# A fourth pair by seven products in the later blocks, with its mixed weights made in the first block

## What is computed

```python
xn = layernorm(x)                                  # (2048, 1024)
s = silu(xn @ w_gate.T)                            # 2752 columns
s[the 1376 smallest |s| of each token] = 0
a = (s * (xn @ w_up.T)) @ w_down.T
h = relu(xn @ up_w) ** 2                           # 2048 columns
shared = h @ down_w
route = sum of the two largest of xn @ gate_w
routed = ((xn @ fc1_w) @ expert_w * route) @ fc2_w
y = x + a + layernorm(shared + routed) * gamma + beta
```

## Time and profile before

| | before |
|---|---|
| median of three runs | 2335.38 us |
| the profiled execution, its own time | 2335.83 us |
| its span, first to last instruction | 2333.7 us |
| granted TensorE clock | 1.000 |
| TensorE matmul busy | 2317.7 us, 99% |
| VectorE busy | 1634.8 us, 70% |
| ScalarE busy | 1086.9 us, 47% |
| GpSimd busy | 829.3 us, 36% |
| chain that ended last | TensorE 93%, DMA 3%, VectorE 1%, SyncE's queue 1%, GpSimd 1% |
| moved by DMA | 558.43 MB, mean 239 GB/s |

### The profile page before, as it was taken

How to read it: one execution, slowest core, us unless ns; L and a number is a source line. 1 busy time by engine, 2 the same in 40 slices (tenths; PEclk the granted TensorE clock), 3 DMA queues, 4 the chain that set the end, 5 groups by cost and what they waited for, 6 DMA issues and landing times.

```text
span 2333.7 us, 27748 instructions
## 1 busy us (share of the span) xinstructions
PE 2317.7 (99%) x10504; PEld 1927.2 (83%) x10504; DVE 1634.8 (70%) x1810; ACT 1086.9 (47%) x1253; POOL 829.3 (36%) x682
## 2 busy tenths in 40 slices
PE   8999999999999999999999999999999999999999
PEld 6888888888877888888888888888888888888887
DVE  4349999976265989897334598898723568989850
ACT  3247776223233787722124387761213448785110
POOL 5467878796444021123024321304004413030500
PEclk9999999999999999999999999999999999999999
DMA  7798878878898666665778766665667865556555
GB/s 277 280 394 294 292 245 311 293 243 310 287 363 302 206 196 191 204 201 180 234 237 277 249 194 193 195 209 189 207 219 255 279 221 195 193 192 214 180 190 180
DMA packets 191047, 558.43 MB, mean 239 GB/s; under 512 B 20161, under 2 KB 29377, under 8 KB 190913
## 3 DMA queue, kind: packets, MB, share of 16 engines
q1 hardware_dynamic: 190912, 556.65, 71.0%
HBM read 429.62 MB, written 126.94 MB: 238 GB/s over the span
## 4 chain that ended last, share of the span: by engine, by line
PE 93%; DMA 3%; DVE 1%; SPq 1%; POOL 1%; ACT 0%; issue 0%; DVEq 0%; ACTq 0%
PE bank L945 30%; PE bank L947 30%; PE bank L946 30%; PE bank L965 2%; DMA mixed_w<-mixes 1%; DMA split_w<-w 1%; DMA w<-mixed_w 1%; PE bank L956 1%; POOL w L732 0%; SPq L565 0%; SPq L569 0%; PE bank L1038 0%; PE bank L1039 0%; DMA raw<-w_gate_dram 0%; POOL w L735 0%
## 5 line engine op out<-in xcount | busy, mean ns | idle before, releaser
L1292 DVE TENSOR_SCALAR_CACHE_REDUCE junk_v<-mag,cand 128x2816 bf16<-128x2816 f32 x248 | 780.3, 3146 | 8.8
L786 ACT ACTIVATE junk_s<-mag,cand 128x2816 uint8<-128x2816 f32 x248 | 655.4, 2643 | 222.2 <-DVE cand L1284 195.7
L945 PE MATMUL bank<-w,tok 128*128 128x512 f32 (+1 forms) x952 | 365.8, 384 | 1.8 <-DMA w<-split_w 1.7
L947 PE MATMUL bank<-w,tok 128*128 128x512 f32 (+1 forms) x952 | 364.3, 383 | 0.0
L946 PE MATMUL bank<-w,tok 128*128 128x512 f32 (+1 forms) x952 | 364.1, 382 | 0.0
L732 POOL TENSOR_TENSOR w<-raw,w 128x512 fp32r<-128x512 f32 (+1 forms) x196 | 268.1, 1372 | 77.5 <-ACT w L774 67.8
L945 PE MATMUL bank<-w,prod_t 128*128 128x512 f32 x672 | 269.4, 401 | 0.0
L947 PE MATMUL bank<-w,prod_t 128*128 128x512 f32 x672 | 262.8, 391 | 0.0
L946 PE MATMUL bank<-w,prod_t 128*128 128x512 f32 x672 | 261.9, 390 | 0.0
L945 PE MATMUL bank<-tok,w 128*128 128x512 f32 x640 | 249.0, 389 | 0.0
L946 PE MATMUL bank<-tok,w 128*128 128x512 f32 x640 | 249.0, 389 | 0.0
(11 more groups left out here) (149 smaller groups left out, 3728.3 us busy)
## 6 DMA issues: line engine op xcount, KB each, us to landing
w<-split_w SPq DMA_DIRECT2D x516, 512.0 KB, 3.5
split_w<-w SPq DMA_DIRECT2D x192, 512.0 KB, 4.9
w_more<-split_w SPq DMA_DIRECT2D x60, 512.0 KB, 5.2
w<-mixed_w SPq DMA_DIRECT2D x108, 256.0 KB, 3.5
rows<-x_dram SPq DMA_DIRECT2D x32, 512.0 KB, 4.9
raw<-w_down_dram SPq DMA_DIRECT2D x44, 256.0 KB, 3.9
raw<-w_up_dram SPq DMA_DIRECT2D x40, 256.0 KB, 3.1
w<-split_w SPq DMA_DIRECT2D x24, 392.0 KB, 3.5
```

Of the source, the lines that this page charges most:

```text
L786: act.activation(junk_s[:, :, :], mag[:, :, t, :], ACT.Sign, scale=-1.0, bias=cand[:, t:t + 1], accum_out=cnt[:, t:t + 1]).then_inc(counte ...
L945: pe.matmul(out, left[0], right[0], start=first, stop=False)
L947: return pe.matmul(out, left[1], right[0], start=False, stop=last)
L1292: dve.tensor_scalar(junk_v[:, :, :], mag[:, :, t, :], cand[:, t:t + 1], float(1 - (GATED - KEPT)), ALU.is_lt, ALU.add, accum_out=cnt[:, t: ...
```

## The change

In blocks 1 to 3 up 0 and up 1 become a fourth pair (`PAIRS`, `FAST`), right behind the third. The later blocks have 260 granules instead of 248: gate 5, four pairs (8 to 119), latent (120), hidden (128), routed (144), shared 0 and 1 (152), hidden 2 and 3 (168), shared 2 and 3 (184 to 199), up 2 and 3 (200), out (216 to 259). Block 0 keeps its 212.

- The search of a later block begins at 101: bit 0 at 101, then 108, 115, 122, and from there every 2.75 granules to 197; its end is at 199. In block 0 it takes one granule more every eight bits.
- Up 0 and up 1 lie where `hidden` and `squares` will lie. SyncE stores them to `spilled_u` (two of 1 MB) at granule 123 and loads them back at 199; ScalarE's first read of hidden waits for the stores. VectorE gives them their signs with two more `sign_up`, ahead of masks 0 and 1, at 205 and 207.
- S3 and S4 go to `acc`. Their splitting moves to granules 12 and 10, and waits until the last outputs of the block before are stored.
- Sets 8 to 15, of the third and fourth pair, are made in block 0 by GpSimd (`late_mix`), with `raw_more` as the one buffer. Set 8 + n: its four loads at granules 38 + 9n to 41 + 9n, its subtractions at 44 + 9n, its four stores of 256 KB at 46 + 9n. The first load of a set waits until the stores of the set before have landed. The sets of block 1, and `mix_later`, are gone.
- In block 0 ScalarE rounds the high half of granules 54, 57, ... 123; GpSimd keeps the other 92.
- The low halves of the last product of pair 4 (index 3) are made by GpSimd, not VectorE.

The diff, cut to its core:

```diff
-PAIRS = [(("gate", 0), ("gate", 1)), (("gate", 2), ("gate", 3)), (("gate", GC - 2), ("up", GC - 2))]
-FAST = len(PAIRS)
+PAIRS = [(("gate", 0), ("gate", 1)), (("gate", 2), ("gate", 3)), (("gate", GC - 2), ("up", GC - 2)),
+         (("up", 0), ("up", 1))]
+
+FAST = [0, 4, 4, 4]
 FIRST_PAIRS = 2
+UP_PAIR, SPILLED_PAIR = 2, 3
 PRODUCTS = ["A11 B11", "S2 T2", "A12 B21", "S1 T1", "S4 B22", "S3 T3", "A22 T4"]
-PRODUCT_BANK = [[4, 6, 0, 2, 4, 6, 0], [2, 4, 6, 4, 6, 0, 2], [4, 6, 0, 4, 6, 0, 2]]
+PRODUCT_BANK = [[4, 6, 0, 2, 4, 6, 0], [2, 4, 6, 4, 6, 0, 2], [4, 6, 0, 4, 6, 0, 2],
+                [4, 6, 0, 4, 6, 0, 2]]
...
-        steps = _middle + _last
+        steps = [step for step in _middle + _last if step[0] not in sum(PAIRS[:FAST[b]], ())]
...
+            self.fast_at.update({last + 2: (FAST[b] - 1, 5), last + 3: (FAST[b] - 1, 6)})
+            self.signs_at = {end["fast", p, q] + FAST_LAG + 3: (p, q) for p in range(UP_PAIR) for q in (5, 6)}
+            up_end = end["fast", UP_PAIR, 6]
+            self.signs_at[last + 4 if up_end == last else up_end + FAST_LAG + 3] = (UP_PAIR, 6)
+        if later and FAST[b] > SPILLED_PAIR:
+            first = up_end + FAST_LAG + 4
+            steps_at = [first, first + 7, first + 14]
+            steps_at += [last + 3 + (11 * k + 3) // 4 for k in range(BITS + 1 - len(steps_at))]
         else:
-            self.search_from = end[("gate", GC - 2)] + LAG + 1
-        self.search_at = {self.search_from + 3 * k: k for k in range(BITS)}
-        self.search_end = self.search_from + 3 * BITS
+            first = last + 5 if later else end[("gate", GC - 2)] + LAG + 1
+            steps_at = [first + 3 * k + (0 if later else k // 8) for k in range(BITS + 1)]
+        self.search_at = {m: k for k, m in enumerate(steps_at[:BITS])}
+        self.search_from, self.search_end = first, steps_at[BITS]
...
+        self.back_at = end[("shared", 3)] if FAST[b] > SPILLED_PAIR else None
+        read = {("up", c): self.back_at + 5 + 2 * c for c in range(2)} if self.back_at else {}
+        read.update({key: end[key] + LAG for key in end})
+        self.mask_at = {max(self.search_end + 1 + i, read.get(("up", g), 0) + 1): g
...
-GPSIMD_HI = list(range(FIRST_PLAN.search_from, FIRST_PLAN.out0))
+GPSIMD_HI = [m for m in range(FIRST_PLAN.search_from, FIRST_PLAN.out0) if m > 124 or m % 3]
...
-MIX_STORES = {26: 8, 34: 9, 46: 10, 54: 11}
+LATE_SETS = {FIRST_MIXES + n: (0, 38 + 9 * n) for n in range(2 * HALF)}
+LATE_LOADS = [{at + i: (n, i) for n, (b, at) in LATE_SETS.items() for i in range(4) if b == c} for c in range(BLOCKS)]
+LATE_AT = [{at + 6: n for n, (b, at) in LATE_SETS.items() if b == c} for c in range(BLOCKS)]
+LATE_STORES = [{at + 8: n for n, (b, at) in LATE_SETS.items() if b == c} for c in range(BLOCKS)]
...
+def vector_makes(granule):
+
+    return PRODUCTS[granule.key[2]] == VECTOR_LO and granule.key[1] < SPILLED_PAIR
...
-SUMS_LO_AT = {2: 4, 4: 3}
+SUMS_HI_AT = [{}, {10: 4, 12: 3}, {10: 4, 12: 3}, {10: 4, 12: 3}]
+SUMS_LO_AT = [{}, {10: 4, 12: 3}, {10: 4, 12: 3}, {10: 4, 12: 3}]
...
+        sums_acc = {i: [over(f"sums{i}_acc{part}", [P, HALF, 2 * P], F32R, acc_at + 8 * N * (2 * (i - 3) + part))
+                        for part in range(2)] for i in (3, 4)}
+        assert 32 * N == TILES * HID * 4
+
+        def sums_of(b, i):
+
+            return sums_acc[i] if i > 2 and FAST[b] > SPILLED_PAIR else sums[i]
...
+        def late_place(n, i):
+
+            return (raw_more if n in LATE_AT[0].values() else raw)[:, i, :]
...
-            def load_mix(n):
+            def load_late_mix(n, i):
 
                 p, k = n // HALF, n % HALF
-                if n < FIRST_MIXES + 2:
-                    sp.wait_ge(stored, 16 * (MIX_BLOCK * 2 * TILES + 1))
+                if n == FIRST_MIXES:
+                    sp.wait_ge(mixes_made, 4 * FIRST_MIXES)
                 else:
-                    sp.wait_ge(mixes_stored[n % 2], 16 * (n // 2))
-                for i in range(4):
-                    src, width = words_of((PAIRS[p][i // 2], k + i % 2 * HALF))
-                    sp.dma_start(mix_place(n, i), src).then_inc(mix_loaded[n % 2], 16)
-
-            def store_later_mix(n):
-                sp.wait_ge(later_mixes, 4 * (n - FIRST_MIXES) + 4)
-                words = acc[:, 2 * (n % 2):2 * (n % 2) + 2, :].rearrange("p t (i n) -> p t i n", n=N)
-                sp.dma_start(mixed_w[n].rearrange("(t i) p n -> p t i n", i=2), words).then_inc(mixes_stored[n % 2], 16)
+                    sp.wait_ge(late_stored, 64 * (n - FIRST_MIXES))
+                if n in LATE_AT[1].values():
+                    sp.wait_ge(lo_ready, FIRST_PLAN.count)
+                src, width = words_of((PAIRS[p][i // 2], k + i % 2 * HALF))
+                sp.dma_start(late_place(n, i), src).then_inc(late_loaded, 16)
+
+            def store_late_mix(n, i):
+                sp.wait_ge(late_mixes, 4 * (n - FIRST_MIXES) + 4)
+                sp.dma_start(mixed_w[n, i], late_place(n, i)).then_inc(late_stored, 16)
+
+            def spill(b, c):
+
+                for q in (4, 5) if c else (2, 6):
+                    for j in range(2):
+                        bank, value = emptied(b, ("fast", SPILLED_PAIR, q, j))
+                        sp.wait_ge(bank_emptied[bank], value)
+                sp.dma_start(spilled_u[c], prod[:, 4 * c:4 * c + 4, :, :]).then_inc(spilled[c], 16)
+
+            def load_back(b, c):
+
+                sp.wait_ge(spilled[c], 16 * spills(b))
+                sp.dma_start(prod[:, 4 * c:4 * c + 4, :, :], spilled_u[c]).then_inc(up_back[c], 16)
...
-                    sp.wait_ge(mixes_stored[n % 2], 16 * (n // 2 + 1))
+                    if n < FIRST_MIXES:
+                        sp.wait_ge(mixes_stored[n % 2], 16 * (n // 2 + 1))
+                    else:
+                        sp.wait_ge(late_stored, 64 * (n - FIRST_MIXES + 1))
...
                 plan = PLANS[b]
-                if b == MIX_BLOCK:
-                    for n in MIX_LOADS.get(m, ()):
-                        load_mix(n)
-                    if m in MIX_STORES:
-                        store_later_mix(MIX_STORES[m])
+                if m in LATE_LOADS[b]:
+                    load_late_mix(*LATE_LOADS[b][m])
+                if m in LATE_STORES[b]:
+                    for i in range(4):
+                        store_late_mix(LATE_STORES[b][m], i)
+                if plan.back_at:
+                    if m == plan.fast_end + 4:
+                        spill(b, 1)
+                        spill(b, 0)
+                    if m == plan.back_at:
+                        load_back(b, 0)
+                        load_back(b, 1)
...
+            def late_mix(n):
+
+                b11, b21, b12, b22 = (late_place(n, i) for i in range(4))
+                at = 4 * (n - FIRST_MIXES)
+                pool.wait_ge(late_loaded, 64 * (n - FIRST_MIXES + 1))
+                pool.tensor_tensor(b11, b12, b11, ALU.subtract).then_inc(late_mixes, 1)
+                pool.tensor_tensor(b12, b22, b12, ALU.subtract).then_inc(late_mixes, 1)
+                pool.wait_ge(late_mixes, at + 1)
+                pool.tensor_tensor(b22, b22, b11, ALU.subtract).then_inc(late_mixes, 1)
+                pool.wait_ge(late_mixes, at + 3)
+                pool.tensor_tensor(b21, b21, b22, ALU.subtract).then_inc(late_mixes, 1)
...
-                    elif POOL_LO[g] > POOL_LO[g - 1]:
+                    if m in LATE_AT[b]:
+                        late_mix(LATE_AT[b][m])
+                    if b and POOL_LO[g] > POOL_LO[g - 1]:
...
-                if i > 2:
+                if i > 2 and FAST[b] > SPILLED_PAIR:
+                    act.wait_ge(stored, 16 * (b * 2 * TILES + 1))
+                elif i > 2:
                     act.wait_ge(bank_filled, filled(b - 1, ("out", 1, TILES - 1)))
...
                                 act.wait_ge(mixes_stored[n], 16 * (FIRST_MIXES // 2))
+                        if FAST[b] > SPILLED_PAIR and i == 0 and t == 0:
+                            for c in range(2):
+                                act.wait_ge(spilled[c], 16 * spills(b))
...
-            def sign_up(b):
-
-                ks = slice(4 * (GC - 2), 4 * (GC - 1))
-                dve.wait_ge(signs_done, b * (GC + 1) + PLANS[b].signs_before[GC - 2] + 1)
-                for j in range(2):
-                    for q in (4, 5):
-                        bank, value = emptied(b, ("fast", FAST - 1, q, j))
-                        dve.wait_ge(bank_emptied[bank], value)
+            def sign_up(b, g):
+
+                ks = slice(4 * g, 4 * g + 4)
+                dve.wait_ge(signs_done, b * (GC + 1) + PLANS[b].signs_before[g] + 1)
+                if g < 2:
+                    dve.wait_ge(up_back[g], 16 * spills(b))
+                else:
+                    for j in range(2):
+                        for q in (4, 5):
+                            bank, value = emptied(b, ("fast", UP_PAIR, q, j))
+                            dve.wait_ge(bank_emptied[bank], value)
```

(8 more changed lines are left out.)

98 lines of the change are left out of this document (41 added, 57 removed).

## The result

The changed kernel takes 2373.21 us (median of four runs, 2371.22 to 2377.07), the kernel before beside it 2335.45 (four, 2334.80 to 2336.54): a ratio of 1.016, 95% interval 1.0148 to 1.0173. It is slower by 38 us. The forecast was 2347, range 2317 to 2358; the sign was right, the size far off.

The account below looks back on a forecast made before the run. TensorE, busy 99% of the span, was taken as the bound. From 2335.8 us: -16.3 (fewer products), -4.3 (block 1's stalls), +27 (sets in block 0), +3 and +2 (new waits) gave 2347.2, stated as 2347, range 2317 to 2358.

Parts of the forecast that it names:

- Fewer matmuls, -16.3: Up chunks 0 and 1 as a fourth fast pair in three later blocks: 72 fewer matmuls, -16.3 us.
- Block 1's four stalls, -4.3: Early block 1: with the sets gone, its four TensorE stalls vanish and it looks like block 2, -4.3 us.
- Block 0, +27: Eight late sets in block 0: ring losses, first set's small lead and squarings cost +27 us, between +3 and +39.
- the ring: Block 0's late-set cycle through GpSimd, SyncE and DMA queues, one buffer: taken as 28.0 us against TensorE's 24.5 per round.
- ScalarE's third high halves: Block 0's search: every third high half, made by ScalarE behind its counts, costs nothing, with 5 us left as cover.
- The squarings add about 0.5: Block 0: GpSimd's squarings add about 0.5 us to the loss, beside the first set's 2 us.
- VectorE's wait hidden: VectorE's wait for `late_stored` at up 4 comes 15 granules after the last set, so it costs nothing.
- (a): Later blocks, granule 13: S3 and S4 halves on GpSimd delay its low half; 1 us per block, +3 us.
- (b): Later blocks' search and tail: threshold and sign passes delay the first transpose, +0.7 us per block, +2 in all.
- (c): Pair 3's low halves on GpSimd end 1.3 us before their granules; nothing, up to 1 us each block.
- The hidden and half hidden ring: Block 0 rivals: queues serve rounds quickly, about 2323 us, chance 0.31; or 26.5 us per round, 2336 us, chance 0.17.
- The rival of the 358 GB/s rule: Block 0: 358 GB/s binds mixed reads and writes, block 0 loses 43 us, time 2363 us; chance 0.03.

## Why the prediction was wrong in size

- **Fewer matmuls, -16.3.** Right: 72 fewer.
- **Block 1's four stalls, -4.3.** Right in size (with what remains, block 1 is 7.0 shorter: 5.4 of matmuls and 4.3 of stalls, less what pair 3 and others gave back), and wrong in one point: a stall of 0.2 to 0.7 us stays or comes where the first mixed weights are used, in some blocks.
- **Block 0, +27: the failed step, +52.1 measured.** The term priced the ring's excess over 24.5 us per round and took every other cost there as next to nothing: GpSimd's own time ("it fits, with 3.3 us to spare"), ScalarE's high halves, the clock. The stalls came where it said, behind the sets and ended by GpSimd, but the experiments show that a set costs TensorE time when the ring is hidden as well. Of the 52.1 us, 6.3 are ScalarE's share and 45.8 the sets; by kind, 39.1 are stalls and 12.7 half clock. The round was derived as 28.7 and then taken as 28.0. That choice was the wrong way: it was 29.6 in the set looked at and 30.2 on average. Of its legs the stores were faster (7.1 against 8.2), granules until the stores slower (4.2 against 3.4), the burst slower (13.2 against 11.8). Seven rounds lose 40 us against 24.5, so about 15 of the missing 25 are here, and part of it is the next point: the half clock behind the stalls lies within these rounds. How much of it lengthened them isn't shown.
- **Half clock, priced at nothing, 12.7 us.** The page of before, with a granted clock of 1.000, could not show it. The run with stalls of chosen length gives what was needed: 1.6 to 2.9 us for each of its stalls from 2.66 us on.
- **"As the ring doesn't contain TensorE, a lead can't cure it."** At nine granules nothing cured it, but the sentence hid the quantity that decides in general. The lead was there to be read: in the rows of before GpSimd idles 0.72 us per granule, because it is as far ahead as six slots allow, 11.3 us at granule 57, whose low half ends at 178.1 against the prediction's own 189.4 for TensorE. I read it at granules 40 and 45 alone.
- **ScalarE's third high halves at nothing, cover "5 us".** Wrong: 7.6 us without sets, 14.3 with four. They were late not behind the second count of a bit but because ScalarE's counts themselves wait for VectorE's candidate, up to 11.5 us in the changed kernel. In the changed kernel itself, with eight sets, the effect can't be told from the scatter.
- **"The squarings add about 0.5"; VectorE's wait hidden.** Wrong: VectorE waited 30.8 us in six waits for GpSimd's squares. At the end of block 0 the sign read of an up group (L1342) was late: 4.0 us of stall at 518.92 and half clock behind it. That the first made the second by way of a late search is argued, not shown (the short form of that chain, at 248.47 without sets, is in the rows above). The waits' row (us in total, times, longest):

```profile
DVE hidden L1507 <- POOL squares L823: 30.8, 6, 12.1
```

- **(a) Granule 13, +3.** No such stall. **(b) Threshold and first transpose, +0.7 per block.** 0.3 to 0.7: right. **(c) Pair 3 at nothing, at most 1 us per block.** 2.1 us of stall, 2.4 to 3.4 of time. The walk put the low halves 1.3 us ahead of their granules; it left out that the second of two counts falls between high halves. Blocks 1 to 3 gained 10.7 us where -16.3 - 4.3 + 5 = -15.6 was said: their losses were 9.9 and not 5, some 6.3 of them in pair 3, 1.5 at the first transposes, the rest mainly stalls of 0.2 to 0.5 us at the first mixed weights and pair 2's last product. The prediction named as a sign of being wrong that the first transposes don't come 3 to 5.5 us closer together; in blocks 2 and 3 they came only 2.0 and 1.7 closer.
- **SyncE waiting 5 us per round for stores, near 400 GB/s.** The rate was 315 and 300 GB/s in the two stretches with sets. SyncE waited 14.0 us in seven waits, at most 3.1: the four issues themselves take 3.6, and what was left was shorter.

```profile
SPq L629 <- DMA mixed_w<-raw_more: 14.0, 7, 3.1
```

- **Rivals.** The hidden and half hidden ring were wrong. (The quiet ring adds up to 3.4 + 6.5 + 8 + 5.3 = 23.2 us, where the prediction has 23.8; nothing hangs on it.) The rival of the 358 GB/s rule came out nearest in time (2363), not for its reason: the trace has 384 GB/s at 163.4 to 168 us and 368 at 170 to 184, in reads and writes mixed. The rule of "DMA: Bandwidth & Descriptors", section "Where 436 GB/s comes from", in the Trainium skill, puts 358 as the bound of such traffic, and these rows disagree.
- **The range.** Its upper end, 2358, took the term's own bound of +39 and no second effect of a stall. The term was above that bound by 13 us, about what the half clock cost.

What stays open: how the 45.8 us of eight sets divide between the ring, GpSimd's full time with its waits for raw loads, and a feedback through squares and search. That a set takes some 6 us off GpSimd's lead, or off TensorE where there is no lead, is what the runs show. The single parts give 9.4 and 21.6 and don't add up. A second buffer for the sets was not tried, for want of room in that stretch.

## What to carry to other kernels

Read how far the helper engine is ahead, everywhere along the stretch and not at its start: a set that took 6 us was free behind a lead of 8 to 11 us and cost 3 behind one of 1 to 3, and the lead grows back only as fast as the helper outruns the bound engine, its waits for transfers included. Don't put work that feeds the bound engine behind one that waits for a third. Price a stall of the bound engine above its own length: here the clock came back 7 to 14 matmuls late after most stalls of 2.7 us and more.
